# Fifth layer of a transformer kernel: outputs weighed ahead of the projection, x normed on ScalarE, the logarithm ahead of the copies of queries and keys

## The reference, cut to what matters

```python
h = _layernorm(x)
q, k, v = (proj(Wq, bq), proj(Wk, bk), proj(Wv, bv))          # h @ W.T + b, by heads
scores = q @ k.T / sqrt(16)
truth_penalty = sigmoid(truth_gate) * norm(k) * 0.01
logp = log_softmax(scores); entropy = -sum(exp(logp) * logp)
balance_adjustment = sigmoid(balance_gate) * entropy / log(32) * 0.1
order_bonus = sigmoid(order_gate) * arange(32) / 32 * 0.05
justice_adjustment = sigmoid(justice_gate) * (mean(scores) - scores) * 0.1
harmony_smooth = -sigmoid(harmony_gate) * mean(abs(scores[1:] - scores[:-1])) * 0.1
attn = softmax(scores - truth_penalty + balance_adjustment + order_bonus
               + justice_adjustment + harmony_smooth)
x = x + (attn @ v) @ Wo.T + bo
```

## Time and profile before

| | |
|---|---|
| time, median of 3 runs | 2464.33 us (2462.03 to 2466.09) |
| the profiled execution's own time | 2459.65 us |
| its span, first to last instruction | 2457.8 us |
| fifth layer, first normed tile to last sum | 1789.6 to 2024.7 us of the span |
| busy over the whole span | PE 82%, PEld 58%, DVE 76%, ACT 57%, POOL 19% |

### The profile page before, as it was taken

One profiled execution on the slowest core, in us unless ns is written; L12 is line 12 of the kernel. 1 busy time (PEld: TensorE's weight loads), 2 busy tenths in 40 slices (PEclk: granted clock), 3 DMA queues, 4 the chain that ended last, 5 costly groups with the idle time before them and its releaser, 6 DMA issues.

```text
span 2457.8 us, 49875 instructions
## 1 busy us (share of the span) xinstructions
PE 2009.3 (82%) x15486; PEld 1430.1 (58%) x15486; DVE 1862.2 (76%) x5158; ACT 1396.5 (57%) x3709; POOL 473.9 (19%) x561
## 2 busy tenths in 40 slices
PE   7999999999997786666799999999867766676665
PEld 6777777777775554333577677677555543333333
DVE  5588877777776456896678778777457778999997
ACT  1355555556563343443466666666555657777776
POOL 0011111111110000110334334333134430000000
PEclk9999999999998898676899999999968878988898
DMA  2011111111110101000011211111010000000000
GB/s 100 10 31 30 30 30 30 30 30 30 30 27 22 66 1 71 25 1 35 19 57 57 61 55 56 54 37 32 20 27 10 10 9 1 0 0 0 0 0 35
DMA packets 64750, 71.76 MB, mean 29 GB/s; under 512 B 40402, under 2 KB 42131, under 8 KB 63636
## 3 DMA queue, kind: packets, MB, share of 16 engines
q1 hardware_dynamic: 64660, 70.73, 9.9%
HBM read 63.47 MB, written 2.10 MB: 27 GB/s over the span
## 4 chain that ended last, share of the span: by engine, by line
PE 60%; DVE 27%; issue 6%; ACT 5%; DMA 1%; DVEq 0%; POOL 0%; SPq 0%; ACTq 0%; POOLq 0%
PE ps L648 5%; PE ps L619 5%; PE ps L610 4%; PE ps L632 4%; PE ps L680 3%; PE ps L1842 3%; DVE f_ams L2520 3%; DVE f_act L2504 3%; PE ps L1825 2%; PE ps L1782 2%; PE ps L1772 2%; PE ps L581 2%; PE ps L2205 2%; PE ps L1851 2%; DVE d_ks L1624 2%
## 5 line engine op out<-in xcount | busy, mean ns | idle before, releaser
L363 ACT ACTIVATE a_pr<-ps,a_nm 128x257 f32<-128x257 f32 x512 | 238.1, 473 | 182.8 <-DVE a_nm L478 182.8
L486 DVE COPY a_pT<-ps 128x512 f32<-128x512 f32 x256 | 170.3, 686 | 92.6 <-PE ps L648 92.1
L1574 ACT ACTIVATE d_pr<-d_st,d_nm 128x257 f32<-128x257 f32 x256 | 128.2, 502 | 193.7 <-DVE d_nm L1694 176.3
L478 DVE TENSOR_REDUCE a_nm<-ps 128x2 f32<-128x514 f32 x256 | 174.9, 683 | 0.0
L2592 PE MATMUL ps<-f_wt,f_nxT 128*128 128x512 bf16 x512 | 157.1, 462 | 18.2 <-DVE f_act L2504 17.7
L648 PE MATMUL ps<-ident,a_pr 128*128 128x128 f32 x1024 | 160.4, 279 | 0.0
L2616 PE MATMUL ps<-f_wt,f_nhT 128*128 128x256 bf16 x512 | 77.5, 302 | 83.8 <-ACT f_nhT L2430 83.8
L1825 PE MATMUL ps<-d_kc,d_qc 128*128 128x257 f32 x512 | 144.2, 406 | 0.0
L303 POOL TENSOR_TENSOR a_sf<-a_sf,a_ratio 128x256 f32<-128x256 f32 x64 | 39.4, 615 | 507.1 <-DVE a_ratio L507 507.1
L648 PEld LDWEIGHTS ps<-ident,a_pr 128*128 128x128 f32 x1024 | 117.5, 140 | 33.4 <-issue 12.7
L610 PE MATMUL ps<-a_cT,a_wqk 128*128 128x257 f32 x512 | 132.7, 381 | 2.9 <-DVE a_k L451 1.7
(11 more groups left out here) (350 smaller groups left out, 5328.6 us busy)
## 6 DMA issues: line engine op xcount, KB each, us to landing
a_cT<-in_ctx SPq DMA_DIRECT2D x64, 257.0 KB, 2.7
d_cT<-in_ctx SPq DMA_DIRECT2D x64, 257.0 KB, 2.8
f_wf<-in_f_w SPq DMA_DIRECT2D x24, 512.0 KB, 3.8
a_vbd<-a_vself SPq DMA_DIRECT2D x256, 8.0 KB
e_vb<-e_vs SPq DMA_DIRECT2D x256, 8.5 KB
c_wf<-in_c_w SPq DMA_DIRECT2D x3, 1024.0 KB, 8.3
x_all<-in_x SPq DMA_DIRECT2D x1, 2048.0 KB, 7.8
d_wo<-in_d_wo SPq DMA_DIRECT2D x1, 2048.0 KB
```

What stands on the lines that cost most here:

```text
L363: ins = act.activation(pr[j][:, g, :], ps[:, S_BANK[u % 2] + k, S:LK], ACT.Exp, bias=nm[j][:, g:g + 1], accum_out=ssum[j][:, 0, g:g + 1])
L478: dve.tensor_reduce(nm[j][:, 2 * u:2 * u + 2], ps[:, s0:s0 + 2, S:LK], AX.X, ALU.max, negate=True).then_inc(max_ready.sem, 1)
L486: dve.tensor_copy(pT[u][:, :, :, :], ps[:, T_BANK[u % 2], :].rearrange("p (g c q) -> p g c q", g=2, c=2))\
L1574: ins = act.activation(pr[j][:, g, :], st[u][:, k, :], ACT.Exp, bias=nm[u][:, k:k + 1], accum_out=sm[j][:, g:g + 1])
```

## The change

Four things move in the fifth layer:

- `weigh` of t-1 goes ahead of `project` of t+1 on TensorE; `turn_o` goes from behind the first half of the scores to directly behind `project`; `output` goes ahead of the second half of the scores.
- `normal`, the normalisation of x, goes from VectorE to ScalarE, as scale and bias of one activation; VectorE makes the bias, minus mean by reciprocal deviation, once for all tiles (`shift`). In a round it stands between the copies `e_xnT` and `e_pT`.
- ScalarE's logarithm goes from behind `values` to directly behind the first exponential, ahead of `queries_keys`.
- ScalarE's `outputs` goes ahead of `values`.

```diff
@@ scalar
+            def normal(t, first=False):
+                if not first:
+                    act.wait_ge(xT_psum.sem, xT_psum.at(t, 0))
+                act.activation(xn[:, :], x_all[:, t, :], ACT.Identity, bias=shift[:, bass.ds(t, 1)],
+                               scale=rstd_all[:, bass.ds(t, 1)]).then_inc(xn_ready.sem, 1)
...
                 if more:
                     turned(t + 1)
+                if more2:
+                    normal(t + 2)
                 if prev:
                     shares(t - 1)
                 act.wait_ge(exp_in.sem, exp_in.at(t, 1))
                 act.activation(w2[:, :, :], w1[:, :, :], ACT.Exp).then_inc(exp_done.sem, 1)
+                act.wait_ge(ln_in.sem, ln_in.at(t, 1))
+                act.activation(rc[:, LSE, :], rc[:, SE, :], ACT.Ln).then_inc(ln_done.sem, 1)
                 if more:
                     queries_keys(t + 1)
-                    values(t + 1, 1 - j, pair)
-                act.wait_ge(ln_in.sem, ln_in.at(t, 1))
-                act.activation(rc[:, LSE, :], rc[:, SE, :], ACT.Ln).then_inc(ln_done.sem, 1)
                 if prev:
                     outputs(t - 1)
+                if more:
+                    values(t + 1, 1 - j, pair)
                 act.wait_ge(exp_in.sem, exp_in.at(t, 2))
@@ vector
+            dve.scalar_tensor_tensor(shift[:, :], mv_all[:, :, 0], -1.0, rstd_all[:, :], ALU.mult, ALU.mult)\
+                .then_inc(bias_ready.sem, 1)
...
-                if more2:
-                    normal(t + 2)
@@ tensor
                     turn_x(t + 1)
-                    project(t + 1)
                 if prev:
                     weigh(t - 1, 1 - j, pair)
                 if more:
-                    project_v(t + 1)
-                    score(t + 1, 0)
+                    project(t + 1)
                 if prev:
                     turn_o(t - 1)
                 if more:
+                    project_v(t + 1)
+                    score(t + 1, 0)
                     norms(t + 1)
-                    score(t + 1, 1)
                 if prev:
                     output(t - 1)
+                if more:
+                    score(t + 1, 1)
```

More of the change, by code:

```diff
@@ L1942, in gated_attention @@
         r2 = sb("e_r2", [P, NH])
+        shift = sb("e_shift", [P, NT])
         w_loaded = shared("w_loaded", 16 * 10, 1)
-        sig_done, zeroed, bias_ready = signal("e_sig_done"), signal("e_zeroed", 5), signal("e_bias_ready", 2)
+        sig_done, zeroed, bias_ready = signal("e_sig_done"), signal("e_zeroed", 5), signal("e_bias_ready", 3)
         yb_psum, yb_ready = signal("e_yb_psum"), signal("e_yb_ready")
@@ L2062, in outputs, with step @@
                     .then_inc(oT_ready.sem, 1)
-            def step(t, j, pair, prev=True, more=True):
+            def step(t, j, pair, prev=True, more=True, more2=True):
                 if more:
                     turned(t + 1)
+                if more2:
+                    normal(t + 2)
                 if prev:
@@ L2081, in step @@
                     scores(t + 1)
+            normal(0, True)
             turned(0)
+            normal(1)
             queries_keys(0)
@@ L2087, in scalar @@
             step(0, 0, None, prev=False)
-            with act.Fori(0, NT // 2 - 1) as i:
+            with act.Fori(0, NT // 2 - 2) as i:
                 step(i * 2 + 1, 1, i + 1)
                 step(i * 2 + 2, 0, i + 1)
-            step(NT - 1, 1, NT // 2, more=False)
+            step(NT - 3, 1, NT // 2 - 1)
+            step(NT - 2, 0, NT // 2 - 1, more2=False)
+            step(NT - 1, 1, NT // 2, more=False, more2=False)
             shares(NT - 1)
@@ L2131, in added, with step @@
                 add_to_x(dve, n, t, ps[:, Y_BANK, 0:HID])
-            def step(t, prev=True, more=True, more2=True):
+            def step(t, prev=True):
                 link.at(t)
@@ L2178, in vector @@
             step(0, prev=False)
-            with dve.Fori(1, NT - 2) as t:
+            with dve.Fori(1, NT) as t:
                 step(t)
-            step(NT - 2, more2=False)
-            step(NT - 1, more=False, more2=False)
             scaled(NT - 1)
```

## The result

The changed kernel takes 2496.89 us (median of four, 2490.40 to 2500.13) against 2463.18 us (2461.57 to 2466.09) of the kernel before on the same chip: a ratio of 1.0132, 95% interval 1.0107 to 1.0157. It is slower, as forecast, but by 33.7 us and not by 10, and 8 us beyond the range. The profiled execution took 2494.25 us, 34.6 more than that of before.

What follows compares the result with a forecast made beforehand. Order and waiting bound the kernel, then TensorE: 12.14 + 1.34 = 13.48 us, plus 0.90 for the clock, 14.38 a round; 14 rounds add 9.8 us to 2459.65, the median 4.7 above: 2474 us, range 2446 to 2489.

Steps and rivals of the forecast that it cites:

- Bound and order: Steady loop: no engine is full, order and waiting set 13.68 us a tile; after the change TensorE bounds, without slack.
- TensorE's slack ahead of `e_pr`: TensorE's wait before the transposes of `e_pr`, 1.54 us a tile, which the change was to spend.
- The waits: TensorE idle 1.43 us ahead of the weighing, about 2.0 ahead of the value projection; VectorE's 1.70 at L2123 gone.
- The normalisation: On ScalarE between `e_xnT` and `e_pT`: 0.50 us in the queue, 0.36 to 0.9 as limits.
- The sum at the clock of before: TensorE's round at the present clock: 12.14 + 1.34 = 13.48 us, 0.20 under the present 13.68.
- The logarithm: On ScalarE ahead of the copies of queries and keys: costs nothing at the present clock, some tenths at full clock.
- the rival with a longer load: Each ScalarE table load holds it 1.28 us more, `e_pr` 0.4 us late a round: 2467 us; chance 0.02.
- The clock: Behind the wait ahead of the value projection it falls in half of the tiles, slowing norms and output: 0.90 us a round.
- the 0.70 to 0.78 that was named as a sign: Granted clock of the loop expected if the forecast holds, with norms at 1.6 to 1.8 us in about half the tiles.
- the first two tiles: Tiles of before with nothing to weigh: TensorE waits 2.11 us ahead of the value projection, then norms are slow.
- 1.79 us: Cost in a tile where the clock falls: 0.85 on the norms and 0.94 on the output.
- The rival with a low clock in every tile: Clock falls before norms and output each round: 13.48 + 1.79 = 15.27 us, 2486.6 us in all; chance 0.14.

Runs made afterwards that it cites:

- e5: The changed kernel with the logarithm behind the copy of the values again, outputs still copied ahead of the values: 2495.53 us, 1.0109 to 1.0165 of before.
- e1: The changed kernel with five unread matmuls a round added on TensorE ahead of the value projection: 2450.74 us, 0.9946 to 0.9971 of before.
- e10: The kernel before with the weighing moved ahead of the projection and five unread matmuls ahead of the value projection: 2480.01 us, 1.0053 to 1.0102 of before.
- e7: The kernel before with four unread matmuls ahead of the transposes of `e_pr` and four ahead of the value projection: 2441.48 us, 0.9898 to 0.9947 of before.

## Why the prediction missed

- *Bound and order: right.* TensorE's slack ahead of `e_pr` is gone. Not the whole truth: the chain of waits runs along TensorE's own order, with the copies it waits for, in the longer rounds (16.3 to 16.6 us); in those of 15.6, whose projection runs at full clock, it runs from the second scores over VectorE's sum, the logarithm and the copies to the value projection.
- *The waits: right.* Ahead of the weighing 18.4 / 12 = 1.53 us where 1.43 was reckoned; ahead of the value projection 24.8 / 12 = 2.07 where 2.0 was. VectorE's wait for the weighing went and a larger one came. The normalisation costs 0.49 us of ScalarE's queue (0.50 was reckoned); ScalarE's timeline of after:

```profile
1912.63 0.59 ACT L2025 ACTIVATE e_xn<-x_all,e_shift,rstd_all 128x256 f32 x1
1913.12 0.59 ACT L2063 ACTIVATE e_pT<-ps 128x512 f32<-128x512 f32 x1
...
1921.85 1.28 ACT L2089 ACT_TABLE_LOAD   x1
1923.14 0.63 ACT L2089 ACTIVATE e_pr<-e_f 128x512 f32<-128x512 f32 x1
```

- *The sum at the clock of before: right.* 9.74 of work (before) and 3.84 of waiting (after) are 13.58; 13.48 was the sum. This is put together from two traces; no run shows the change at that clock.
- *The logarithm: right for the time, by e5.* A table load costs 1.28 us and `e_pr` follows 0.01 us behind (the rows just shown), so the rival with a longer load falls.
- *The clock: wrong, and it is the whole miss.* The step that failed is "Two tiles showed it and the first round with a weighing did not; the new order lies between them, so I take half, 0.90". Measured is 16.25 - 13.58 = 2.67 us; over 14 rounds the difference of 1.77 makes 25 us, and the time missed the forecast by 22.9. Two errors are in it. First the share: norms and output ran at half clock in every tile, not in half of them, and the clock of the loop, 0.62, is under the 0.70 to 0.78 that was named as a sign. The gap of the change is that of the first two tiles, 2.07 against 2.11 us without work; the turned outputs stand at its front, as the weighing had, but take up only some 0.3 us of it where the weighing took 0.66 and left 1.58. There was no "between". Second the price: 1.79 us counted norms and output alone. Over twelve tiles the groups give, a tile, output 4 x (667 - 452) = 0.86 us, norms 8 x (353 - 246) = 0.86, value projection 4 x (575 - 404) = 0.68, scores 0.44 (16.7 / 12.5 less 10.8 / 12, by busy time), the transposes of `e_pr` 4 x (434 - 360) = 0.30, less the projection's 16 x (405 - 367) = 0.61: 2.5 in all. The weighing, (12.3 - 8.3) / 12 = 0.33, and some 0.1 for the transposes of x come on top, and since neighbouring groups overlap, they sum to more than the 2.67 of busy time. The trace of before had the value projection of its second tile at 1.13, because there the clock fell only behind it; here it falls within it in three rounds of four and ahead of it in the fourth, and it stays low into the next projection.
- The rival with a low clock in every tile was the right mechanism, at 2486.6 us; it too had only the 1.79.

The Trainium skill, page "TensorE: Matmul & The Clock Gate", section "A second HAM failure mode: psum-queue depth-cycling", says of another kernel, in bf16, that short pauses between groups of matmuls make the clock swing between half and full speed and cost throughput. The trace agrees on the swing: in every round shown of the change the granted clock reaches 1.00 in the projection and is 0.50 over scores, norms and output.

## What to carry to other kernels

Work that stands in a wait of TensorE may be what keeps its clock up: before moving it out, look in the trace for a place where the same gap is already empty, and price every matmul from there into the next dense stretch at the lower level (1.2 GHz in place of 2.4), not the two nearest. When a change of order loses time, compare busy time and idle time of the same instructions first, and fill the gap with matmuls that nobody reads: it tells clock from waiting in one run (e1), and may be a gain to keep. Then look whether the clock is up over the whole round: in e10 it was up behind the filled gap and low ahead of it. Undoing one part at a time is no proof while the clock is down, since the next wait takes its place.

## What was not expected of the hardware

- Matmuls that nobody reads made a tuned kernel 0.8% faster (e7) and the change 1.8% (2450.74 against 2496.89).
- The fall does not cost all forms the same: value projection 1.13 to 2.07 us, output 1.13 to 2.05, norms 0.98 to 1.86, but scores 0.45 to 0.68 and transposes of `e_pr` 0.66 to 1.11.
- The gap of 1.5 us ahead of the weighing, with the projection behind it, left the loop of e1 at a granted clock of 0.90; with 2.1 us open ahead of the value projection as well it was 0.62. In three rounds of four of the change the clock is still up in that gap and falls only within the value projection behind it. What in the second gap makes the difference, its length or the work behind it, was not separated.
